# ScalarE's row sums read into a PSUM bank, and copied to SBUF once a quarter

## What is computed

```python
e = jnp.stack([tbl_f[ids[:, f]] for f in range(32)], axis=1)      # 512 x 32 x 64
left = einsum('bpd,pde->bpe', e[:, idx_i, :], W)                  # 496 pairs
z = sum(left * e[:, idx_j, :], axis=-1)                           # 512 x 496
h = concatenate([z, dense_ctx], axis=1)
h = maximum(h @ W_top1 + b_top1, 0)
h = maximum(h @ W_top2 + b_top2, 0)
y = h @ W_top3
```

## Time and profile before

| | |
|---|---|
| time, median of 3 runs | 240.29 us (237.7 to 240.94) |
| span of the profiled execution | 281.1 us |
| TensorE, VectorE, ScalarE, GpSimd busy | 227.2, 187.5, 205.6, 137.2 us |
| mean granted TensorE clock, as a share of full speed | 0.921 |

### The profile page before, as it was taken

One profiled execution on the slowest core, in us unless ns is written; L12 is line 12 of the kernel. 1 busy time (PEld: TensorE's weight loads), 2 busy tenths in 40 slices (PEclk: granted clock), 3 DMA queues, 4 the chain that ended last, 5 costly groups with the idle time before them and its releaser, 6 DMA issues.

```text
span 281.1 us, 6932 instructions
## 1 busy us (share of the span) xinstructions
PE 227.2 (81%) x2228; PEld 149.4 (53%) x2228; DVE 187.5 (67%) x196; ACT 205.6 (73%) x1665; POOL 137.2 (49%) x169
## 2 busy tenths in 40 slices
PE   4524978878778897997978969968789979999865
PEld 4412936434555535374638525546547436664765
DVE  4910357678556695684776677877467699999613
ACT  0000049999875897999999565999899889999930
POOL 4773054565454562564462555454363657786000
PEclk9975897999989977997997999999897999999979
DMA  6998972111011100010110011011110100000000
GB/s 192 380 362 275 339 240 58 21 20 20 18 22 16 23 20 14 16 27 14 22 23 13 19 20 26 11 21 19 18 19 18 23 15 2 5 0 4 0 0 2
DMA packets 11084, 16.54 MB, mean 59 GB/s; under 512 B 3737, under 2 KB 3737, under 8 KB 10921
## 3 DMA queue, kind: packets, MB, share of 16 engines
q1 hardware_dynamic: 7208, 12.17, 12.6%
q0 software_dynamic: 3840, 3.94, 7.5%
HBM read 16.10 MB, written 0.00 MB: 57 GB/s over the span
## 4 chain that ended last, share of the span: by engine, by line
PE 41%; ACT 35%; issue 13%; DVE 8%; another core or an unknown queue 2%; DVEq 0%; ACTq 0%
ACT prod_act L459 35%; PE left L656 16%; PE left L646 10%; PE left L626 5%; PE zsum L670 4%; DVE prod_col L529 3%; DVE prod_act L507 3%; PE left L732 2%; PE left L636 1%; PE zsum L616 1%; PE zsum L696 1%; PE left L716 1%; PE spread_more L616 1%; DVE sums L559 0%
## 5 line engine op out<-in xcount | busy, mean ns | idle before, releaser
L459 ACT ACTIVATE prod_act<-prod_act 128x64 f32<-128x64 f32 x832 | 199.1, 240 | 19.0 <-DVE prod_act L507 10.2
L410 POOL DMA_INDIRECT rows<-tbl_dram,ids x120 | 113.7, 947 | 114.0 <-DVE prod_col L529 52.0
L459 ACT ACTIVATION_READ_ACCUMULATOR prod_act<-prod_act 128x1 f32 x832 | 155.6, 187 | 6.1 <-issue 5.6
L656 PE MATMUL left<-xt,w 64*128 64x128 f32 x992 | 78.1, 299 | 16.9 <-issue 11.4
L656 PEld LDWEIGHTS left<-xt,w 64*128 64x128 f32 x992 | 71.3, 208 | 36.4 <-issue 19.0
L529 DVE TENSOR_TENSOR prod_col<-left,xt 128x1024 f32<-128x1024 f32 x62 | 73.7, 1219 | 24.4 <-remote 16.5
L646 PE MATMUL left<-w,xt 64*128 64x512 f32 x264 | 72.3, 652 | 5.4 <-DVE prod_act L507 4.9
L507 DVE TENSOR_TENSOR prod_act<-left,rows 128x1024 f32<-128x1024 f32 x52 | 62.3, 1218 | 17.9 <-PE left L646 9.7
L646 PEld LDWEIGHTS left<-w,xt 64*128 64x128 f32 x264 | 23.1, 196 | 31.0 <-issue 12.0
L670 PE MATMUL zsum<-prod_col,selector 128*32 128x256 f32 x496 | 35.2, 396 | 3.5 <-DVE prod_col L529 2.8
L459 ACT ACT_TABLE_LOAD x1 | 1.3, 1283 | 38.9 <-DVE prod_act L507 38.9
(11 more groups left out here) (40 smaller groups left out, 92.7 us busy)
## 6 DMA issues: line engine op xcount, KB each, us to landing
w<-pair_w_dram SPq DMA_DIRECT2D x32, 256.0 KB, 5.1
rows<-tbl_dram,ids POOLq DMA_INDIRECT x120
z<-tbl_dram SPq DMA_DIRECT2D x4, 256.0 KB
w<-tbl_dram SPq DMA_DIRECT2D x4, 256.0 KB
w<-w_top_dram SPq DMA_DIRECT2D x1, 1024.0 KB
w<-w_top_dram SPq DMA_DIRECT2D x1, 512.0 KB
dense<-dense_t_dram SPq DMA_DIRECT2D x16, 2.0 KB
ids<-ids_dram SPq DMA_DIRECT2D x1, 64.0 KB, 2.6
```

What stands on the lines that cost most here:

```text
L410: pool.indirect_dma_start(out=rows[:, part % ROW_BUFS, n, h, :], out_offset=None, in_=a[f"tbl_{f}"], in_offset=bass.IndirectOffsetOnAxis(a ...
L459: op = act.activation(p, p, ACT.Copy, accum_out=sums[:, part % 2, k:k + 1])
L656: mm = pe.matmul(slot(item)[:, col:col + PB], w[own, g, i, :], xt[own, part % 2, moving_of(unit, half), :], start=True, stop=True)
```

## The change

`act_sums` is a new name for the bank `spread_more`: 512 columns, 256 for even and 256 for odd quarters. Each of the 832 ACTIVATEs now names a column of it as its sum's output, instead of a column of `sums`. After a quarter's 13 groups ScalarE waits for its own last read (`act_added`), and copies the 8 x 26 columns from the bank to their places in `sums` with one ACTIVATE that raises `act_copied`. The fold waits for `act_copied` in place of `act_added`. VectorE's ring of product buffers still goes by `act_added`.

```diff
+        act_sums = spread_more
...
+        act_copied = sem("act_copied")
...
-                        op = act.activation(p, p, ACT.Copy, accum_out=sums[:, part % 2, k:k + 1])
+                        op = act.activation(p, p, ACT.Copy, accum_out=act_sums[:, 2 * P * (part % 2) + k:2 * P * (part % 2) + k + 1])
                     op.then_inc(act_added, 1)
+                act.wait_ge(act_added, NACT * (part + 1))
+                whole = act_sums[:, 2 * P * (part % 2):2 * P * (part % 2) + 2 * P].rearrange("p (s k) -> p s k", k=32)
+                act.activation(sums[:, part % 2, :2 * P].rearrange("p (s k) -> p s k", k=32)[:, :, :2 * NACT],
+                               whole[:, :, :2 * NACT], ACT.Copy).then_inc(act_copied, 1)
...
             def fold(part):
-                pe.wait_ge(act_added, NACT * (part + 1))
+                pe.wait_ge(act_copied, part + 1)
```

## The result

| | before | after |
|---|---|---|
| time, median | 240.62 us (4 runs) | 211.19 us (4 runs) |
| ratio, with its 95% interval | | 0.88 [0.8715, 0.8885] |
| profiled execution: span | 281.1 us; a second one, below, 239.0 | 209.5 us (its own time 211.38) |
| ScalarE and TensorE busy (before: second trace) | 200.0, 202.6 us | 173.5, 196.8 us |
| pair of ACTIVATE and read | 0.239 us | 0.197, then 0.205 us |

The change takes 12% off the time, 29.4 us. I had forecast 234.5 and a range down to 227.5; the outcome lies outside it. Some executions are over 1.5% slower than the fastest of their kernel, at a lower granted TensorE clock (of the changed kernel's four, 214.41 us at 0.983 against about 211 us at 0.991 and 0.992); they don't count in the ratios, but do in the medians.

The account below looks back on a forecast made before the run. ScalarE was taken to set the end, ahead of a fixed 11.45 us tail. From 240.3 us, a gain of 5.8 us (lag less 0.7, between -0.7 and +12.5) gave 234.5 us, range 227.5 to 242.

Parts of the forecast that it names:

- step 1: Read's destination to PSUM, 832 times: pair from 0.239 to 0.207 us, 26.6 us less over all pairs.
- rivals A: ScalarE's pair stays at 0.239 us and only the copies cost: about 241.2 us; chance 0.25.
- B: Alternating destinations end ScalarE's overlap, each ACTIVATE waits for the read's write: about 315 us; chance 0.06.
- step 3: ScalarE's four copies, 0.36 us each plus about 0.05 of waiting; the last adds 0.41 us to the path.
- The reading of the 281.1 us trace: Profiled kernel before: its 37.4 us of issue gaps mostly absent in unprofiled runs, where ScalarE is busier and ends last.
- The sum for the profiled execution: Whole profiled run: 281.1 us, less 4.35 at ScalarE's end, plus 0.41 for the last copy, given as 277.1 us.
- lag - 0.7: Unprofiled gain from how far ScalarE's queue trails the last products, lag 0 to 13.2 us; 5.8 us taken.
- the signs that I had named: Changed trace: read-to-ACTIVATE step 0.065 us, copies about 0.36, ScalarE waiting for VectorE near the end, last fold 4.6 behind.
- C: Six product buffers held VectorE, and through it TensorE, back in unprofiled runs: time below 227.5 us; chance 0.04.

Follow-up runs that it names:

- second trace: The kernel before, unchanged, profiled again: 240.88 us, span 239.0 us.
- The run with the saving in the last quarter alone: The kernel before with 8 of the 16 sums of each ScalarE group left out in the last quarter only: 227.25 us, ratio 0.9498.

## Why the prediction was wrong

**The price of the pair (step 1) was right.** I took 0.207 us, from VectorE's fixed cost, within bounds of 0.144 and 0.331; measured are 0.197 to 0.205. With it rivals A (0.239 us as before) and B (a slower pair) fall. The destination matters for the read alone: with the ACTIVATE's own output in PSUM too, its step stays at 0.15 us. The Trainium skill's figures ("Perfetto Trace Analysis", "Optimizing Scalar/DVE Operations") of about 93 ns on SBUF and 51 ns on PSUM are what the step behind the read shows here, 0.093 and 0.051 us.

**The copy (step 3) was right in size, 0.34 us, and wrong in its wait**: it starts 0.74 us behind the last read's start, where the read's record was 0.19 us before, since the records grow. The pause also lets the records start short again, which returns some 0.5 us a quarter (64 pairs x 0.008).

**The reading of the 281.1 us trace was half right.** The 37.4 us of issue were absent in the second trace (1.4% of the chain), as I had assumed for the runs, and ScalarE was busier there: it never paused in its 198.75 us. (The sum for the profiled execution comes to 277.2, not 277.1 us.)

**The step that failed is "So the gain is lag - 0.7: from -0.7 to +12.5 us".** It let a faster ScalarE end earlier, but kept the last product where it was. Two sentences carried that: products "come no earlier", and of the first folds "TensorE is not listed as waiting for ScalarE there". Both held in the disturbed trace alone. There TensorE reached its first two folds so late (at 105.1 and 165.8 us, against 77.7 and 127.4) that ScalarE had already summed. In an undisturbed execution TensorE waited 13.2 us in these two folds and VectorE 5.0 us for buffers, and the last product came 17.6 us earlier after the change (211.9 to 194.3): 14.3 us by less waiting of TensorE, 3.3 us by faster matmuls.

The formula itself, for a saving that lies wholly at the end, is not far off. In the second trace of before the lag was 226.65 - 3.83 - 211.9 = 10.9 us, for which it gives 10.2. The run with the saving in the last quarter alone gained 12.3, and its tail is about 2.5 us shorter (215.06 to 224.8), which the formula had no term for. That this is near my upper bound of 12.5 us is luck. The change spread its saving over all quarters.

Of the signs that I had named, the step and the copy's 0.34 us came. ScalarE did not wait for VectorE near the end, and the last fold stands 5.4 us behind the last product, not 4.6.

**The rival that came true is C**, to which I gave 0.04: ScalarE's pace came back through TensorE and VectorE. I named the ring of buffers for it, but the folds did most of it, and the gain went far beyond the 12.5 us that I allowed for it. I dismissed it because "in the profile, VectorE waits nowhere for ScalarE", again a fact of one trace, after having written that the other runs were another regime. My own numbers pointed to it: 199.2 + 11.45 left 29.6 us for the start and all waits, less than the 40.2 us before the first ACTIVATE in the trace. An engine that hardly pauses has a backlog behind it, and then each pair counts. With my own price, 832 x 0.032 = 26.6 us less and 1.7 for the copies, the sum would have been about 215 us, with TensorE's 227 us of busy time in that trace as the doubt.

Where the 29.5 us of span went, second trace of before against the change: first ACTIVATE 27.90 to 27.28, -0.6; ScalarE's run 198.75 to 171.98 (27.28 to 199.26), -26.8; last copy to the fold, +0.4; the tail from the fold on, 12.3 to 9.8, -2.5. The tail's part is TensorE's clock. The same view as above of before (second trace) and then of after, from the last product to the fold and from the fold to the end:

```profile
211.90:226.65 14.75, 4.63 (x42) 4.43 (x40) 3.72 (x8) 14.75 (x124) 0.00 (x0) 0.83 0.00 1
226.65:239.00 12.35, 9.34 (x84) 8.90 (x84) 3.15 (x11) 0.00 (x0) 0.00 (x0) 0.78 0.01 1
```

```profile
194.30:199.65 5.35, 4.57 (x41) 4.38 (x40) 3.67 (x7) 5.30 (x50) 0.00 (x0) 1.00 0.00 0
199.65:209.50 9.85, 6.86 (x84) 6.42 (x84) 3.15 (x11) 0.00 (x0) 0.00 (x0) 1.00 0.01 2
```

Before, TensorE idled 10.17 us ahead of the last fold, and the tail ran partly at the lower of its two clock levels (mean 0.78, 9.34 us busy). Now it idles 0.81 us, and the same matmuls run at the full 2.4 GHz in 6.86 us.

## What to carry to other kernels

If an engine's busy time, the time before its first work and the tail behind its last add up to the measured time, it is the bound. The others' lateness is then its doing, through every wait on it in the middle of their queues, and a saving that is spread over its work comes back in full, down to the next engine's floor (here 26.8 us of its run gave 29.4). Where the saving stands matters: in the last quarter alone, behind the waits that had held the others, only 12.3 of 24.9 us came back. Check that the trace's span fits the runs before taking a "nobody waits here" from it; where it doesn't, argue from the sum over the runs. Measure the floor directly by leaving out half of the suspect's work: here it gave 206 us at once.

## What the hardware showed unexpectedly

- A ScalarE accumulator read costs 0.093 us into SBUF and 0.051 us into PSUM, and the 64-column ACTIVATE from SBUF before it about 0.15 us whichever of the two it writes.
- With the read into PSUM the records of both grow by 0.008 us a pair, to 0.80 and 0.71 us, and the pair then goes from 0.197 to 0.205 us (0.170 to 0.178 with 32 columns); the step from ACTIVATE to read takes the difference, 0.146 to 0.154 us. The wait ahead of each copy sets it back. Whoever waits for such a read waits the grown record.
- A 208-column copy to SBUF by ScalarE steps in 0.240 us from PSUM and 0.282 us from SBUF.
- One profiled execution of the kernel before was 17% longer than the runs, with 13.3% issue on its chain; another, of the same program, was not.
